# Where the shared expert's tiles stand, a third place for x tiles, logits copied by ScalarE, and a fifth place for gate matrices

## The chip, the core and the metric

The kernel runs on one core of one Trainium2 chip. The metric is the device time in microseconds (us) of one execution; lower is better. Five engines work side by side, each through its own queue of instructions in order: TensorE (PE, with its weight loads as PEld), VectorE (DVE), ScalarE (ACT), GpSimd (POOL) and SyncE (SP, which here only issues DMAs). They wait for each other by semaphores that the kernel sets out by hand. Whatever engine issues a transfer, the core's 16 DMA engines carry it.

## The reference, cut to what matters

The input is two sequences of 1024 tokens, 512 wide. An attention-like layer comes first, then a mixture of 64 experts with a shared expert beside them:

```
x = x + attention(layernorm(x)) @ Wo       # cumulative sum over time, norm over a whole sequence
h = layernorm(x)
logits = h @ w_router.T;  four best of 64 experts per token;  softmax over the four
for each expert (at most C=64 tokens of it):
    y = (silu(h_e @ w_gate[e]) * (h_e @ w_up[e])) @ w_down[e]     # 512 -> 384 -> 512, float32
    combined[tokens of e] += y * weight
combined += (silu(h @ w_sh_gate) * (h @ w_sh_up)) @ w_sh_down     # shared expert, all tokens
out = x + combined
```

Each expert's three float32 matrices are 768 KB (786,432 bytes) each, so the 64 experts bring 151 MB from memory through the DMA engines once.

## The kernel before, in words

The program has two halves. The first takes sequence 0 and then sequence 1, in tiles of 128 tokens (8 a sequence): norm, transposed copy, three projections, scan over time, output projection, residual, second norm, router logits. While the second norm of sequence 0's tiles is made, the first norm of sequence 1's tiles is made beside it: an x tile is loaded by SP into one of two places `xin`, normed, turned by TensorE and split. SP loads these tiles and the tiles for the residual (`ring`, four places) in one order (lines 409 to 420), and before each ring tile it waits for the store of the tile that stood there. In sequence 1's second norm, VectorE copies the router's logits out of PSUM (line 1005, called for tile n-2 after the norm of tile n), and then picks the best experts and builds sorted lists of tokens, a long chain of small VectorE operations.

The second half takes the experts in 32 pairs, two pairs (u = 0 and 1) in each of 16 groups j; pair p = 2j + u. For a pair, tokens are gathered from memory by an indirect DMA of POOL (`xg`, line 605), turned, multiplied with the pair's gate and up matrices (line 1550), silu and product, turned again, multiplied with the down matrices (line 1571), weighted, merged where two experts of the pair share a token (lines 1532 to 1536), and added to the output in memory by an indirect DMA of POOL with addition (line 614). The additions are serial: each waits for the landing of the one before (`added`).

The matrices come through SP's queue, each as two pieces of 384 KB (line 246). A down matrix stands in one of three places; gate and up matrices have a fourth, `extra`. From pair 5 on, SP goes down-of-pair p-2, gate-of-p, up-of-p, and before each it waits until TensorE has finished with what stood in that place (`load_matrix`, `load_down`). What stands behind a waiting transfer in SP's queue waits with it.

The shared expert works on 16 tiles of 128 tokens. The last four of the order (LEAD = 4: tiles 12 to 15 of the token order, kept in SBUF, items 0 to 3 of the shared work) are done around the start: their results are added to the residual x2 in SBUF and stored by `store_late` (line 735), the fourth at the end of group 0. The other twelve (SHARED) are done one to a group, in groups 1 to 12; their turned inputs come back from memory (`xS`), their outputs are gathered in `yS`, three at a time, and added to the output by one POOL DMA (line 627) in groups 3, 6, 9 and 12, in the same serial chain as the pairs' additions. Groups with a shared tile merge in two float32r parts (`y`, `y_low`), the others in whole float32 (`y_whole`).

```
def in_parts(j, u):
    return j + u <= SHARED
BATCHES = range(3, SHARED + 1, 3)
```

Of the kernel before, what the change touches and what calls it, by code (L numbers as in the profile page):

```python
# [25 lines left out]
F32R = mybir.dt.float32r  # L26
# [30 lines left out]
LATE = TOKENS // P - LEAD  # L57


def moe_block(nc, x, wr, wk, wv, wo, decay, gn_w, gn_b, w_router, w_gate, w_up, w_down,  # L60
# [4 lines left out]
    with ExitStack() as ctx:  # L65
# [72 lines left out]
        xin = [tile(f"xin{u}", [P, D], at=xin_at + u * 2048) for u in range(2)]  # L138
# [22 lines left out]
        logits = tile("logits", [P, TILES, E + 4], at=logits_at)  # L161
        top8 = tile("top8", [P, TILES, 8])
# [6 lines left out]
        best = tile("best", [P, C])  # L169
        cand = tile("cand", [E, 2 * C], at=xin_at + 1024)  # L170
# [20 lines left out]
        y, y_low = tile("y", [P, D], F32R, at=ramp_at), tile("y_low", [P, D], F32R, at=logits_at)  # L191
# [4 lines left out]
        y_whole = tile("y_whole", [P, D], at=ramp_at)  # L196
# [14 lines left out]
        def place(p, k):  # L211

            return p % (SLOTS + 1 if k < 2 else SLOTS)

        def uses(p, k):

            return p // (SLOTS + 1 if k < 2 else SLOTS)
# [8 lines left out]

        def in_parts(j, u):

            return j + u <= SHARED

        def gate_up(p, e, k):
            return matrix(p, e, k).rearrange("p (c n) -> p c n", c=KC)
# [6 lines left out]

        def fill_matrix(eng, p, k, experts=range(2)):  # L240

            for e in experts:
                src = (w_gate, w_up, w_down)[k][p * 2 + e].rearrange("(p c) n -> p (c n)", p=P)
                for h in range(PIECES):
                    cols = slice(h * W // PIECES, (h + 1) * W // PIECES)
                    eng.dma_start(matrix(p, e, k)[:, cols], src[:, cols]).then_inc(w_full[k][place(p, k)], 16)  # L246
# [5 lines left out]
        BATCHES = range(3, SHARED + 1, 3)  # L252
# [27 lines left out]
        xin_full, ring_full = sem2("xin_full"), [sem(f"ring_full{i}") for i in range(RING)]  # L280
# [32 lines left out]
        w_full = [[sem(f"w_full{k}_{i}") for i in range(SLOTS + (k < 2))] for k in range(3)]  # L313
# [13 lines left out]
        def xin_place(n):  # L327
# [4 lines left out]
            return xin[n % 2], xin_full[n % 2], 16 * ((n - 4) // 2 + 1 - (n >= TILES))  # L332
# [38 lines left out]
        def _(sp):  # L371
# [38 lines left out]
            for n in range(RING):  # L410
                load_x(n, xc_place)
            for n in range(RING, TILES):
# [1230 lines left out]
```

## Time and profile before

| | us |
|---|---|
| median of 3 runs (lowest, highest) | 733.49 (730.72, 734.45) |
| the profiled execution, its own time | 732.06 |
| its span in the profile | 729.9 |
| TensorE busy in the span | 680.2 (93%) |
| VectorE busy | 332.8 (46%) |
| GpSimd busy | 219.0 (30%) |
| ScalarE busy | 159.7 (22%) |

Durations are taken from the one profiled execution, and are set against its own 732.06 us. The span runs from the first to the last traced instruction. A DMA share is the mean busy share of the 16 DMA engines in a stretch, and can come out a little over 1. In a list of instructions a row is: start in us, busy us, engine, line of the kernel, operation, output<-inputs, and in brackets the idle time of that engine before it and what ended it. "SPq", "POOLq" and "ACTq" are the queues' own issuing of DMAs. Chain rows are the work that ended last, followed back from the end.

### The profile page before, as it was taken

What the parts mean: (1) busy time and instruction counts of PE and PEld (TensorE: products, weight loads), DVE (VectorE), ACT (ScalarE), POOL (GpSimd) and SP (SyncE); (2) the same over time, 40 slices, a digit from 0 to 9 for tenths busy, and PEclk for the clock granted to TensorE, in tenths of its full rate; (3) what the DMA queues carried; (4) which work ended last, traced back from release to release, by engine and by line L of the source; (5) the groups of instructions that cost most, each with busy time, mean ns of one, the idle gap of its engine ahead of it and who ended that gap; (6) DMA issues with size and microseconds to landing.
All of it is one profiled execution on the core that took longest, in us unless ns stands there. A gap on an engine that the chain in (4) does not pass through costs nothing.

```text
span 729.9 us, 9206 instructions
## 1 busy us (share of the span) xinstructions
PE 680.2 (93%) x3229; PEld 411.9 (56%) x3229; DVE 332.8 (46%) x817; ACT 159.7 (22%) x251; POOL 219.0 (30%) x209
## 2 busy tenths in 40 slices
PE   3999999899999998999999999999999999997783
PEld 2687878788787854554554554554554554543330
DVE  5887567648987692233323323323323323322111
ACT  4832215523111221112112112112112112111110
POOL 4637455326646313012121221112121221112101
PEclk9999999589999999999999999999999999999997
DMA  9101006710877888499999999999999999999992
GB/s 324 57 7 53 1 15 237 240 42 1 292 244 270 294 299 278 156 357 378 392 390 375 363 378 376 392 357 379 381 390 377 363 378 374 393 359 378 382 353 33
DMA packets 79996, 202.69 MB, mean 278 GB/s; under 512 B 10403, under 2 KB 10531, under 8 KB 79568
## 3 DMA queue, kind: packets, MB, share of 16 engines
q1 hardware_dynamic: 64160, 169.25, 61.2%
q0 software_dynamic: 8928, 21.33, 12.2%
q10 hardware_dynamic: 6864, 11.54, 4.3%
q8 instruction: 26, 0.43, 0.2%
q14 instruction: 18, 0.15, 0.1%
HBM read 178.66 MB, written 23.59 MB: 277 GB/s over the span
## 4 chain that ended last, share of the span: by engine, by line
PE 65%; SPq 11%; DVE 9%; DMA 3%; issue 2%; POOL 1%; ACT 1%; ACTq 0%; DVEq 0%; POOLq 0%
PE bank L1550 18%; PE bank L1338 12%; SPq L246 11%; PE bank L1571 9%; PE bank L1471 8%; PE bank L1490 5%; PE bank L1360 3%; DMA w_sb<-in_L_ffn_w_up 2%; PE bank L1498 2%; PE bank L1558 1%; DVE key L1045 1%; PE bank L1385 1%; DVE best L1044 1%; PE bank L1461 1%; DVE state L956 1%
## 5 line engine op out<-in xcount | busy, mean ns | idle before, releaser
L614 POOL DMA_INDIRECT out_dram<-ym,midx x32 | 51.3, 1603 | 313.5 <-DVE ym L1235 198.9
L1550 PE MATMUL bank<-w_sb,xT 128*64 128x384 f32 x768 | 129.8, 489 | 6.8 <-DMA w_sb<-in_L_ffn_w_up 4.3
L1338 PE MATMUL bank<-x_hi,w_parts 128*128 128x512 f32 x384 | 123.4, 404 | 4.5 <-DVE x_lo L940 3.2
L1571 PE MATMUL bank<-w_sb,guT 128*64 128x512 f32 x384 | 89.7, 603 | 6.2 <-issue 6.2
L1550 PEld LDWEIGHTS bank<-w_sb,xT 128*64 128x64 f32 x768 | 53.3, 137 | 70.4 <-issue 58.0
L1338 PEld LDWEIGHTS bank<-x_hi,w_parts 128*128 128x128 f32 x384 | 74.6, 195 | 22.1 <-DVE x_lo L940 4.0
L1338 PE MATMUL bank<-x_lo,w_parts 128*128 128x512 f32 x192 | 75.4, 401 | 0.0
L1171 DVE TENSOR_TENSOR gu<-sg,bank 128x384 f32<-128x384 f32 x32 | 17.7, 553 | 124.8 <-issue 117.9
L1471 PE MATMUL bank<-sh_sb,xS 128*128 128x384 f32 x192 | 63.9, 486 | 0.0
L1571 PEld LDWEIGHTS bank<-w_sb,guT 128*64 128x64 f32 x384 | 28.2, 138 | 55.9 <-issue 55.0
L1471 PEld LDWEIGHTS bank<-sh_sb,xS 128*128 128x128 f32 x192 | 35.7, 191 | 22.3
L1490 PE MATMUL bank<-sh_sb,guT 128*128 128x512 f32 x96 | 45.1, 605 | 0.0
L833 ACT ACTIVATE sg<-bank 128x384 f32<-128x384 f32 x32 | 15.7, 491 | 131.9 <-PE bank L1550 131.9
L1550 PE MATMUL bank<-extra,xT 128*64 128x384 f32 x256 | 43.0, 489 | 0.0
L852 ACT ACTIVATE y<-bank,wcol 128x512 fp32r<-128x512 f32 x25 | 17.2, 687 | 116.6 <-PE bank L1571 116.6
L1176 DVE COPY guT<-bank 128x384 f32<-128x384 f32 x32 | 17.7, 554 | 54.1 <-PE bank L1558 54.1
L1338 PEld LDWEIGHTS bank<-x_lo,w_parts 128*128 128x128 f32 x192 | 37.6, 196 | 7.9
L605 POOL DMA_INDIRECT xg<-xw_dram,pair_idx x32 | 31.8, 993 | 28.3 <-DVE pair_idx L1217 10.3
L511 POOL TENSOR_TENSOR v_sb<-v_sb,inv 128x512 f32<-128x512 f32 x16 | 20.8, 1299 | 62.7 <-ACT v_sb L678 61.6
L1235 DVE COPY ym<-bank 128x512 f32<-128x512 f32 x32 | 22.0, 689 | 35.2 <-PE bank L1533 29.6
L487 POOL TENSOR_TENSOR rstd<-var_eps,minus_half 128x1 f32<-128x1 f32 x34 | 21.1, 620 | 45.2 <-DVE var_eps L904 45.2
L1182 DVE TENSOR_TENSOR gu<-sg,bank 128x384 f32<-128x384 f32 x16 | 8.8, 552 | 56.2 <-issue 50.5
(179 smaller groups left out, 954.3 us busy)
## 6 DMA issues: line engine op xcount, KB each, us to landing
w_sb<-in_L_ffn_w_down SPq DMA_DIRECT2D x128, 384.0 KB
w_sb<-in_L_ffn_w_gate SPq DMA_DIRECT2D x96, 384.0 KB
w_sb<-in_L_ffn_w_up SPq DMA_DIRECT2D x96, 384.0 KB
extra<-in_L_ffn_w_gate SPq DMA_DIRECT2D x32, 384.0 KB
extra<-in_L_ffn_w_up SPq DMA_DIRECT2D x32, 384.0 KB
ring<-in_L_attn_x SPq DMA_DIRECT2D x14, 256.0 KB, 3.7
xt_dram<-xwT ACTq DMA_DIRECT2D x12, 256.0 KB, 3.2
xS<-xt_dram SPq DMA_DIRECT2D x12, 256.0 KB
```

The costliest lines, as they stand in the source:

```text
L246: eng.dma_start(matrix(p, e, k)[:, cols], src[:, cols]).then_inc(w_full[k][place(p, k)], 16)
L487: pool.tensor_tensor(rstd[n % 4][:, :], var_eps[n % 4][:, :], minus_half[:, :], ALU.pow).then_inc(rstd_ready, 1)
L511: pool.tensor_tensor(v_sb[u][:, :], v_sb[u][:, :], inv[:, c, t], ALU.mult).then_inc(vscaled, 1)
L605: pool.indirect_dma_start(out=xg[j % 2][u][:, :], out_offset=None, in_=xw_dram[:, :], in_offset=bass.IndirectOffsetOnAxis(ap=pair_idx[:, 2 ...
L614: pool.indirect_dma_start(out=out[:, :], out_offset=bass.IndirectOffsetOnAxis(ap=midx[j % 3][u][:, :], axis=0), in_=ym[u][:, :], in_offset ...
L1235: dve.tensor_copy(ym[u][:, :], pair_bank(j, u)[:, :]).then_inc(ym_ready[u], 1)
L1338: ins = pe.matmul(ps[u][:, :], w, xp, start=(n == 0), stop=(n == len(parts) - 1))
L1360: ins = pe.matmul(ps_y[n % 4][:, :], o, w, start=(m == 0), stop=(m == len(parts) - 1))
L1471: ins = pe.matmul(ps[:, 0:I], xS[t % 2][:, c, :], sh_gu[w][:, c, :], start=(c == 0), stop=(c == KC - 1))
L1490: ins = pe.matmul(ps_d[1][:, :], guT[1][:, c, :], sh_dn[:, c, :], start=(c == 0), stop=(c == IC - 1))
L1550: ins = pe.matmul(ps[e * C:(e + 1) * C, 0:I], xT[:, c, e * C:(e + 1) * C], gate_up(2 * j + u, e, k)[:, c, :], start=(c == 0), stop=(c == K ...
L1571: ins = pe.matmul(pair_bank(j, u)[e * C:(e + 1) * C, :], guT[0][:, c, e * C:(e + 1) * C], down(2 * j + u, e)[:, c, :], start=(c == 0), sto ...
```

## The change

Four things are changed.

1. The twelve shared tiles go from groups 1 to 12 to groups 3 to 14 (FIRST = 3). Groups 1 and 2 have none; the batches of `yS` go from groups 3, 6, 9, 12 to groups 5, 8, 11, 14.
2. x tiles of sequence 1 have three places (the third is half of the old `state` room, so its first load waits for the scan of sequence 0 to end), and each is loaded one place earlier in SP's order.
3. The logits of sequence 1 are copied by ScalarE (`take_logits` there), right after the turned copy of the next tile, and no longer by VectorE.
4. Gate matrices get a fifth place, `spare`, made of four parts of half a matrix. Two parts (expert 0 of the pair) lie over the room of `ramp` and of the lists' work tiles, and may be filled once the token lists are made and the weights are stored; two (expert 1) lie over the residual tiles of the four late tiles, and may be filled when all four are stored (`late_stored` at 64). `y`, `y_low` and `y_whole` move to other room. In the last group the tokens' row of pair 31 is made before that pair's down product.

```diff
-            return p % (SLOTS + 1 if k < 2 else SLOTS)
+            return p % (SLOTS + 2 - k)
+        def has_shared(j):
+            return j == 0 or FIRST <= j < FIRST + SHARED
+        def item(j):
+            return LEAD + j - FIRST if j else TAIL
         def in_parts(j, u):
-            return j + u <= SHARED
+            return has_shared(j + u)
+        def piece(p, e, k, h):
+            if k == 0 and place(p, k) == SLOTS + 1:
+                return spare[e][h][:, :]
+            return matrix(p, e, k)[:, h * W // PIECES:(h + 1) * W // PIECES]
-        BATCHES = range(3, SHARED + 1, 3)
+        BATCHES = range(FIRST + 2, FIRST + SHARED, 3)
@@ SP: a matrix waits for the pair that last stood in its place
-                if k < 2 and p > SLOTS:
-                    sp.wait_ge((g_ready, u_ready)[k][p % 2], p // 2 - 1)
+                last = p - (SLOTS + 2 - k)
+                if k < 2 and last >= 0:
+                    sp.wait_ge((g_ready, u_ready)[k][last % 2], last // 2 + 1)
@@ SP: x tiles
+            sp.wait_ge(out_done, STEPS)
+            load_x(TILES + 2, xin_place)
             for n in range(RING, TILES):
                 sp.wait_ge(xn_ready, TILES + n - RING + 1)
-                load_x(TILES + n - 2, xin_place)
+                load_x(TILES + n - 1, xin_place)
                 sp.wait_ge(x2_stored[n % RING], 16)
                 sp.wait_ge(xw_ready, n - RING + 1)
                 load_x(n, xc_place)
@@ SP: the experts' matrices from pair 4 on
-            for p in range(4, 2 * GROUPS):
-                if p > 4:
-                    load_down(p - 2)
-                if p % 2 and 2 <= (p - 3) // 2 < SHARED:
-                    load_shared_tile((p - 3) // 2)
+            fill_piece(sp, 4, 0, 0, 0)
+            sp.wait_ge(wgt_stored, 16 * SEQS)
+            fill_piece(sp, 4, 0, 0, 1)
+            load_matrix(4, 1)
+            sp.wait_ge(late_stored, 16 * LEAD)
+            for h in range(PIECES):
+                fill_piece(sp, 4, 1, 0, h)
+            for p in range(5, 2 * GROUPS):
+                load_down(p - 2)
+                if p % 2 and 2 <= (p - 1) // 2 - FIRST < SHARED:
+                    load_shared_tile((p - 1) // 2 - FIRST)
                 for k in range(2):
                     load_matrix(p, k)
@@ POOL: the batch of three shared tiles
                 if j in BATCHES:
-                    pool.wait_ge(yS_ready, j + LEAD)
+                    pool.wait_ge(yS_ready, j - FIRST + 1 + LEAD)
@@ ACT: logits of sequence 1
+            def take_logits(n):
+                act.wait_ge(logit_ready, n + 1)
+                if n == TILES:
+                    act.wait_ge(mask_ready, 2)
+                act.activation(logits[:, n % TILES, 0:E], ps_l[n % 2][:, 0:E], ACT.Copy).then_inc(logit_copied, 1)
@@ DVE
                 second_norm(n)
-                if n > TILES + 1:
-                    take_logits(n - 2)
             pick(1, 0)
-            take_logits(2 * TILES - 2)
-            take_logits(2 * TILES - 1)
             pick(1, 1)
@@ PE, last group
                 merge_pair(j, 0)
+                turn_tokens_of_pair(j, 1)
                 if last:
                     down_pair(j, 1)
-                turn_tokens_of_pair(j, 1)
-                if last:
                     merge_pair(j, 1)
```

Order of SP's DMAs before, from the last pieces of pair 3's gate and up matrices on (`extra`k`e`: matrix kind k, expert e; `w_sb`n: place n of three; "x4" is both experts in two pieces each):

```order
L246 DMA extra11_194<-in_L0_ffn_w_up 128x768 x2
L246 DMA extra10_193<-in_L0_ffn_w_up 128x768 x2
L246 DMA w_sb0_195<-in_L0_ffn_w_gate 128x768 x4
L246 DMA w_sb0_195<-in_L0_ffn_w_up 128x768 x4
L246 DMA w_sb0_195<-in_L0_ffn_w_down 128x768 x4
L246 DMA w_sb1_196<-in_L0_ffn_w_gate 128x768 x4
L246 DMA w_sb1_196<-in_L0_ffn_w_up 128x768 x4
L246 DMA w_sb1_196<-in_L0_ffn_w_down 128x768 x4
```

And after, at the same place (`spare`eh: expert e, half h):

```order
L265 DMA extra11_199<-in_L0_ffn_w_up 128x768 x2
L265 DMA extra10_198<-in_L0_ffn_w_up 128x768 x2
L265 DMA spare00_184<-in_L0_ffn_w_gate 128x768
L265 DMA spare01_185<-in_L0_ffn_w_gate 128x768
L265 DMA w_sb0_200<-in_L0_ffn_w_up 128x768 x4
L265 DMA spare10_186<-in_L0_ffn_w_gate 128x768
L265 DMA spare11_187<-in_L0_ffn_w_gate 128x768
L265 DMA w_sb0_200<-in_L0_ffn_w_down 128x768 x4
L265 DMA w_sb0_200<-in_L0_ffn_w_gate 128x768 x4
L265 DMA w_sb1_201<-in_L0_ffn_w_up 128x768 x4
L265 DMA w_sb1_201<-in_L0_ffn_w_down 128x768 x4
```

The gate matrices of pair 4 now go to the spare place, two pieces ahead of that pair's up matrices and two behind them; the down matrices of pair 3, which stood right behind pair 4's up matrices, now stand behind the last two pieces, and so behind the wait for the four late stores.

POOL's DMAs at the end before, from pair 24's addition on (`ym`u: result of pair u of a group; `yS`: three shared tiles; `xg`: gathers):

```order
L614 DMA out_dram<-ym0_182,midx00_155 2048x512
L627 DMA out_dram<-yS_190 128x3x512
L614 DMA out_dram<-ym1_183,midx01_156 2048x512
L605 DMA xg10_200<-xw_dram,pair_idx_153 128x576
L605 DMA xg11_201<-xw_dram,pair_idx_153 128x576
L614 DMA out_dram<-ym0_182,midx10_157 2048x512
L614 DMA out_dram<-ym1_183,midx11_158 2048x512
L614 DMA out_dram<-ym0_182,midx20_159 2048x512
L614 DMA out_dram<-ym1_183,midx21_160 2048x512
L614 DMA out_dram<-ym0_182,midx00_155 2048x512
L614 DMA out_dram<-ym1_183,midx01_156 2048x512
```

And the same stretch after:

```order
L650 DMA out_dram<-ym0_188,midx00_156 2048x512
L650 DMA out_dram<-ym1_189,midx01_157 2048x512
L641 DMA xg10_205<-xw_dram,pair_idx_154 128x576
L641 DMA xg11_206<-xw_dram,pair_idx_154 128x576
L650 DMA out_dram<-ym0_188,midx10_158 2048x512
L650 DMA out_dram<-ym1_189,midx11_159 2048x512
L650 DMA out_dram<-ym0_188,midx20_160 2048x512
L663 DMA out_dram<-yS_195 128x3x512
L650 DMA out_dram<-ym1_189,midx21_161 2048x512
L650 DMA out_dram<-ym0_188,midx00_156 2048x512
L650 DMA out_dram<-ym1_189,midx01_157 2048x512
```

The last batch of shared tiles stood seven additions before the end, and stands three before it now.

VectorE's order in the second norm of sequence 1 before, for one tile (`x_second`: residual, `xw`: normed tile):

```order
L924 TENSOR_SCALAR xw_101<-x_second,mv_116,rstd_124 128x512
L1005 COPY logits<-bank 128x64
L995 SCALAR_TENSOR_TENSOR x_second<-bank,grstd,x_second 128x512
L914 BN_STATS stats<-x_second 128x6
L915 BN_AGGR mv_118<-stats 128x2
L904 TENSOR_SCALAR var_eps_122<-mv_118 128x1
L924 TENSOR_SCALAR xw_102<-x_second,mv_117,rstd_125 128x512
```

And after:

```order
L970 TENSOR_SCALAR xw_102<-x_second,mv_117,rstd_125 128x512
L1041 SCALAR_TENSOR_TENSOR x_second<-bank,grstd,x_second 128x512
L960 BN_STATS stats<-x_second 128x6
L961 BN_AGGR mv_119<-stats 128x2
L950 TENSOR_SCALAR var_eps_123<-mv_119 128x1
L970 TENSOR_SCALAR xw_103<-x_second,mv_118,rstd_126 128x512
```

The copy of the logits, which needs TensorE's router product, no longer stands between a norm and the next residual.

## Rows read from the trace of the kernel before

**Rows 1.** The page: share of the DMA engines in 40 slices of 18.2 us.
```profile
DMA  9101006710877888499999999999999999999992
```

**Rows 2.** Stretches: us, busy of PE, PEld, DVE, ACT, POOL; clock, DMA share, GB/s.
```profile
130.50:151.00 20.50, 18.38 (x68) 15.40 (x69) 10.67 (x32) 9.07 (x13) 6.11 (x12) 0.50 0.67 227
...
296.00:304.00 8.00, 8.00 (x48) 3.40 (x46) 2.13 (x6) 0.49 (x1) 0.00 (x0) 1.00 0.01 2
...
360.00:708.00 348.00, 335.98 (x1671) 165.95 (x1671) 103.09 (x301) 56.97 (x99) 69.34 (x52) 1.00 1.05 378
```

**Rows 3.** The chain that ended last, towards its end: start, us, what.
```profile
597.48 0.79 SPq L246
...
677.78 13.66 DMA w_sb<-in_L_ffn_w_up
```

**Rows 4.** TensorE's instructions: two like groups' starts, and pair 29's down product.
```profile
309.18 5.38 PE L1550 MATMUL bank<-w_sb,xT 128*64 128x384 f32 x32
...
336.55 5.38 PE L1550 MATMUL bank<-w_sb,xT 128*64 128x384 f32 x32
...
696.62 4.49 PE L1571 MATMUL bank<-w_sb,guT 128*64 128x512 f32 x12 [2.33 <-issue]
```

**Rows 5.** The page: the shared expert's products, busy and mean ns of one.
```profile
L1471 PE MATMUL bank<-sh_sb,xS 128*128 128x384 f32 x192 | 63.9, 486 | 0.0
...
L1490 PE MATMUL bank<-sh_sb,guT 128*128 128x512 f32 x96 | 45.1, 605 | 0.0
```

**Rows 6.** SP's queue around group 0: pair 4's gates, pairs 3 and 5 later.
```profile
284.33 1.87 SPq L246 DMA_DIRECT2D w_sb<-in_L_ffn_w_gate  x4
...
304.57 1.75 SPq L246 DMA_DIRECT2D w_sb<-in_L_ffn_w_down  x4
306.37 1.98 SPq L246 DMA_DIRECT2D w_sb<-in_L_ffn_w_gate  x4
```

**Rows 7.** The fourth late store: its issue, and POOL's addition that waits for it.
```profile
310.39 0.34 ACTq L735 DMA_DIRECT2D out_dram<-x_second  x1
...
317.40 1.63 POOL L614 DMA_INDIRECT out_dram<-ym,midx  x1 [26.61 <-DMA out_dram<-x_second]
```

**Rows 8.** The page's DMA issues: engine, count, KB each, median us to landing.
```profile
out_dram<-x_second ACTq DMA_DIRECT2D x8, 256.0 KB, 3.1
```

**Rows 9.** TensorE at the first gathered tile of the experts.
```profile
280.00 0.72 PE L1498 MATMUL bank<-ident,xg 128*128 128x128 f32 x4 [0.78 <-ACT guT L880]
```

**Rows 10.** POOL: around the last batch of shared tiles, and the last additions.
```profile
639.02 1.62 POOL L614 DMA_INDIRECT out_dram<-ym,midx  x1 [8.37 <-DVE ym L1235]
647.47 1.40 POOL L627 DMA_DIRECT2D out_dram<-yS  x1 [6.83 <-issue]
660.40 1.66 POOL L614 DMA_INDIRECT out_dram<-ym,midx  x1 [11.53 <-DVE wcol L1260]
...
688.84 1.56 POOL L614 DMA_INDIRECT out_dram<-ym,midx  x1 [8.94 <-DVE ym L1235]
...
714.70 1.56 POOL L614 DMA_INDIRECT out_dram<-ym,midx  x1 [8.54 <-DVE ym L1235]
721.21 1.55 POOL L614 DMA_INDIRECT out_dram<-ym,midx  x1 [4.95 <-issue]
```

**Rows 11.** VectorE's waits from 102 to 147: us, times, longest.
```profile
DVE stats L914 <- DMA xin<-in_L_attn_x: 2.0, 2, 1.1
```

**Rows 12.** ScalarE's and VectorE's split of sequence 1's x tile 12.
```profile
128.10 0.60 ACT L659 ACTIVATE x_hi<-bank 128x512 fp32r<-128x512 f32 x1 [0.40 <-ACT xwT L721]
...
129.54 0.68 DVE L940 TENSOR_TENSOR x_lo<-bank,x_hi 128x512 fp32r<-128x512 f32 x1
```

**Rows 13.** TensorE's last projection, VectorE's residual of tile 15, its second pick.
```profile
242.20 0.39 PE L1360 MATMUL bank<-wo_hi,out_lo 128*128 128x512 f32 x1
...
246.46 0.74 DVE L995 SCALAR_TENSOR_TENSOR x_second<-bank,grstd,x_second 128x512 f32<-128x512 f32 x1
...
254.06 0.60 DVE L1012 MAX8 top<-logits 128x8 f32<-128x64 f32 x4
```

More of the change, by code:

```diff
@@ L137, in moe_block @@
         xin_at, xn_at, xw_at = room(K4), room(K4), room(K4)
-        xin = [tile(f"xin{u}", [P, D], at=xin_at + u * 2048) for u in range(2)]
+        xin = [tile(f"xin{u}", [P, D], at=a) for u, a in enumerate((xin_at, xin_at + 2048, st_at + 2048))]
         xn = [tile(f"xn{u}", [P, D], at=xn_at + u * 2048) for u in range(2)]
@@ L190, in moe_block @@
         guT = [tile(f"guT{n}", [P, IC, P], at=None if n < 1 else st_at + 2048) for n in range(2)]
-        y, y_low = tile("y", [P, D], F32R, at=ramp_at), tile("y_low", [P, D], F32R, at=logits_at)
+        y_at = xw_at + 2 * I * 4
+        assert y_at + 2 * 2048 <= top8_at and top8_at + W * 2 <= best_end
+        y_whole = tile("y_whole", [P, D], at=y_at)
+        y, y_low = tile("y", [P, D], F32R, at=y_at), tile("y_low", [P, D], F32R, at=y_at + 2048)
+        spare = [[tile(f"spare{e}{h}", [P, W // PIECES], at=a) for h, a in enumerate(places)]
+                 for e, places in enumerate(((ramp_at, top8_at), (inv_at + 8192, inv_at + 8192 + W * 2)))]
         ym = [tile(f"ym{u}", [P, D]) for u in range(2)]
@@ L311, in moe_block @@
         tok_ready, tok_turned, idx_ready = sem("tok_ready"), sem("tok_turned"), sem("idx_ready")
-        w_full = [[sem(f"w_full{k}_{i}") for i in range(SLOTS + (k < 2))] for k in range(3)]
+        w_full = [[sem(f"w_full{k}_{i}") for i in range(SLOTS + 2 - k)] for k in range(3)]
         xg_full = [sem2(f"xg_full{r}") for r in range(2)]
@@ L417, in _ @@
                 load_x(n, xc_place)
-            for n in range(2 * TILES - 2, 2 * TILES):
-                sp.wait_ge(xn_ready, n - 1)
-                load_x(n, xin_place)
+            sp.wait_ge(xn_ready, 2 * TILES - 3)
+            load_x(2 * TILES - 1, xin_place)
             def load_second_rows(c):
@@ L811, in _ @@
                 turned_xw(n)
+                if n > TILES:
+                    take_logits(n - 1)
                 store_residual(n)
@@ L854, in group @@
             def group(j):
-                first, last, shared = j == 0, j == GROUPS - 1, j <= SHARED
+                first, last, shared = j == 0, j == GROUPS - 1, has_shared(j)
                 silu(j, 0)
@@ L1262, in group @@
             def group(j):
-                first, last, shared = j == 0, j == GROUPS - 1, j <= SHARED
+                first, last, shared = j == 0, j == GROUPS - 1, has_shared(j)
                 columns(j, 0)
@@ L1530, in merge_pair @@
                 if in_parts(j, u):
-                    pe.wait_ge(ylow_ready[u], j + 1)
+                    pe.wait_ge(ylow_ready[u], sum(in_parts(i, u) for i in range(j + 1)))
                     pe.matmul(pair_bank(j, u)[:, :], same[u][:, :], y[:, :], start=True, stop=False)
@@ L1575, in group @@
             def group(j):
-                first, last, shared = j == 0, j == GROUPS - 1, j <= SHARED
+                first, last, shared = j == 0, j == GROUPS - 1, has_shared(j)
                 gate_and_up(j, 0)
```

46 lines of the change are left out of this document (27 added, 19 removed).

## The prediction

> **What bounds the kernel now.** I read the page first, then stretches of the span, then the chain that ended last, then the queues. The page's line of DMA shares [rows 1] is the first thing to see: in 22 slices in a row, from about 310 us to 711 us, the 16 DMA engines are 90% busy or more. The stretch from 360 to 708 says how much: DMA share 1.05 at 378 GB/s, with TensorE busy 335.98 of 348 us [rows 2]. So two resources look full at once, and the reader must decide which one sets the end. The chain decides it: up to 597 us it runs over TensorE, from 597.48 on over the issuing of matrices in SP's queue, and from 677.78 over a landing of up matrices [rows 3]. TensorE is ahead of nothing after 597; it has used up the lead that the full places gave it.
>
> A count shows why. A group brings 4 experts x 3 x 786,432 bytes = 9.44 MB of matrices; two gathers of 0.295 MB, two additions of 0.262 MB, one tile of `xS` and a third of a batch of `yS` (0.262 MB each) make it 11.1 MB, which is 29.3 us at 378 GB/s. TensorE needs 27.37 us for a group with a shared tile (309.18 to 336.55 [rows 4]) and some 8 us less without: one tile's products are 63.9/12 + 45.1/16 = 5.3 + 2.8 us [rows 5], so about 19.3 us. The stream of matrices is slower than TensorE in both kinds of groups. Once it runs without a gap, the end is: the time at which it starts to run without a gap, plus its bytes at 378 GB/s, plus what follows the last landings. Where the shared tiles stand changes none of the three by itself; only lost or won DMA time before the stream is full, and the tail, count.
>
> **The fifth gate place and the start of the stream.** Before, SP issues pair 4's gates at 284.33, as soon as pair 0's gate product frees the place, then pair 4's up matrices; the next, pair 3's down matrices, wait for pair 0's down product and go at 304.57, pair 5's gates at 306.37 [rows 6]. Between 296 and 304 the DMA engines do nothing (share 0.01 [rows 2]). From there on the stream is full.
>
> After, half of pair 4's gates (0.79 MB) goes some 10 us earlier, into time in which the engines had room; that gains nothing, since it doesn't bring the full stream forward. Pair 4's up matrices go at about 287 as before. But then SP waits for the four late stores before it issues the other half, and behind that wait stand pair 3's down matrices, pair 5's gates and all that follows. The fourth late store is issued by ScalarE at 310.39 [rows 7]. In the trace POOL's first addition, which waits for the same store, starts at 317.40 [rows 7], but the store then shares the engines with 4.7 MB of matrices. After, it is alone; such stores land 3.1 us after their issue (median of 8 [rows 8]), so at 313.5. That is the bound from below; 317.4, as now, is the one from above. I take 313.5, because the quiet engines are certain.
>
> So the full stream starts at 313.5 instead of 304.57: +8.9 us. It must then also carry the half of pair 4's gates that before was down by then: 0.786 MB / 378 GB/s = +2.1 us. The late store itself (0.262 MB) no longer takes time out of it: -0.7 us. Sum +10.3 us, with bounds +9 and +14. TensorE does not notice at once: pair 2 starts at 309.18 [rows 4], and pair 4 one unshared group later, at about 328.5, while its gates land at about 318. With two unshared groups it then draws faster than the stream supplies, and I expect it to stand waiting for landings from about group 5 on, instead of from group 13 on. Its work is the same; only the place of its idle time moves.
>
> **Gathers beside the extra pieces.** The two early pieces go out right when the token lists are made, beside the first gathers. TensorE's first gathered tile starts at 280.00, 0.78 us after its own work allowed [rows 9], so there is no slack behind the gather. Bounds: 0 and the pieces' whole 0.79 MB, 2.1 us; nearest to the row, which shows the gather and ScalarE's copy arriving together, I take +0.5. The Trainium skill speaks against this placing (DMA: Bandwidth & Descriptors, section Issuing engines are not separate DMA queues): transfers of different issuers run on the same 16 engines and interleave, so another queue is no protection. By that rule the term would be nearer to 2.1 than to 0; no row here shows a gather beside two such pieces.
>
> **The last batch of shared tiles.** POOL's additions are a chain of landings. While the stream is full, an addition issued at 639.02 lets the batch go at 647.47, 8.5 us later; the batch holds the next addition until 660.40, 12.9 us; with idle engines one addition follows the other in 6.5 us (714.70 to 721.21) [rows 10]. Before, the batch of group 12 was long absorbed at the end. After, a batch stands behind the addition of pair 28. That addition starts at 688.84 now; the shared tile's second half (2.8 us [rows 5]) delays its merge: 691.7. Then 8.5 (700.2), 12.9 (713.1, addition of pair 29), 6.5 (719.6), 6.5 (726.1, addition of pair 31), against 721.21 now: +4.9 us on the tail, between 0 (a batch that lands quickly as the stream ends) and +7 (all steps at 8.5). The reordered last merge saves TensorE about a microsecond, which this chain hides.
>
> **Three x places.** VectorE waited 2.0 us for x tiles, twice [rows 11]. Of this only a part comes back: the split of x tile 12 at 129.54 needs ScalarE's copy, which ends at 128.70 [rows 12]. So -0.8 us. Bounds: 0, and a gain through TensorE's clock: from 130.5 to 151 it was granted half (1.2 GHz), with TensorE 18.38 us busy [rows 2]; at full clock that would take up to 9.2 us less. It fell after TensorE had idled between tiles with no projections left to do; VectorE's pace of about 4 us a tile stays, so I expect it to fall again, and take nothing for it.
>
> **Logits on ScalarE.** VectorE's residual of tile 15 starts at 246.46, though its projection ended at 242.59 [rows 13]; the copies of logits, each waiting for a router product, stood in between. Without them it starts up to 3.9 us earlier. ScalarE's seven or eight small copies stand between its turned copies and lie beside TensorE's products. The chain of picking and sorting that starts at 254.06 with the second pick [rows 13] and runs on VectorE to the token lists moves as a whole. Bounds 0 and -3.9; near the row I take -3.4, and lose the rest to turning and routing the last four tiles one after the other.
>
> **Sum.** 10.3 + 0.5 + 4.9 - 0.8 - 3.4 = +11.5 us on the profiled execution's 732.06: 743.5 us (span 741.4). The median of the runs shown is 1.4 us above that execution, which I leave in the range. What a measurement of this kernel can tell from no change is about 0.5%, 3.7 us either way, so 729.8 to 737.2 is the same.
>
> **Rivals.**
>
> 1. Faster, TensorE sets the end. If the 378 GB/s is drawn by TensorE and is not the engines' limit, the late start of the stream is made up, and the idle time of TensorE in the last groups, 348 - 335.98 = 12.0 us [rows 2], goes, since shared tiles now fill it. Span 729.9 - 12.0 - 3.7 (x and logits, less the gathers) + 4.9 = 719.1, time 721. It decides if the DMA rate after 320 rises above 378. For it: TensorE is busy 97% of that stretch. Against: when TensorE starved, after 597, SP's issuing itself was the chain [rows 3], so the queue was full and still gave no more. The Trainium skill would leave it open: DMA: Bandwidth & Descriptors, section Where 436 GB/s comes from, puts the fabric's ceiling at 435 GB/s, which as an estimate would make the 348 us 302. Its page Perfetto Trace Analysis, section Identifying the Most-Contended Engine, also warns of reading the busy share of 16 engines. 7%.
>
> 2. The same: the first half gives more. The clock stays up (half of the bound of 9.2, 4.6 us) and the batch hides (4.9): 743.5 - 9.5 = 734. For it: less waiting for x tiles. Against: VectorE's pace. With smaller parts of both it would end near 737. 17%.
>
> 3. Slower still: the store lands as late as now (+3.9) and the gathers lose 1.6 more: 749. It decides if anything but the two stores of the late tiles uses the engines at 310. 12%.
>
> 4. Slower, by less: the wait for the late stores costs 5 us less, since part of what stood behind it was idle anyway: 738.5. 9%.
>
> The forecast keeps 55%, with its own range 739.5 to 747.5. Faster: rival 1 and a little of 2, 9%. Same: 15%. Slower: the rest, 76%. The range that leaves out at most 2 in 10 reaches down into rival 2 and up to rival 3: 734 to 750.
>
> **What would show it.** DMA share near 0 from about 290 (profile's time, less some 3 us) until after the fourth late store, then 378 GB/s without a gap to the end; SP's down matrices of pair 3 some 7 to 10 us later than 304.57; landing waits of TensorE on L1550's counterpart from group 5 on; POOL's batch behind the fourth addition from the end, and the last addition 5 us later relative to pair 29's down product. VectorE's second pick some 4 us before 254.06. It would be wrong if TensorE waits for no landings in groups 5 to 12, or if the rate goes well above 378 GB/s.

## The result, and the profile after

| | us |
|---|---|
| changed kernel, median of 4 runs (lowest, highest) | 741.32 (739.51, 741.99) |
| kernel before beside it, median of 4 runs (lowest, highest) | 732.46 (730.72, 734.45) |
| ratio, 95% interval | 1.0115 (1.009 to 1.014) |
| profiled execution: its own time, its span | 739.51, 737.7 |

All medians in this document are of fast runs; two runs of the kernel before, at 3876.87 and 797.7 us, are left out.

The change costs 8.9 us where 11.5 were forecast; the interval goes from 6.6 to 10.3 us. The measured time lies in the predicted range. How far the single terms were right is another question, which the experiments answer.

The page's DMA line of the changed kernel, in slices of 18.4 us, answers to [rows 1]:

```profile
DMA  9100007601775995199999999999999999999993
```

The slice with a 1, at about 295 to 313 us, is nearly empty, where before a 4 stood; behind it again an unbroken row of nines. Stretches of the changed kernel, with the columns of [rows 2]:

```profile
130.50:151.00 20.50, 17.37 (x72) 14.18 (x72) 9.13 (x28) 8.20 (x12) 4.91 (x11) 0.67 0.54 192
...
300.00:308.00 8.00, 8.00 (x38) 4.10 (x36) 2.65 (x5) 1.28 (x2) 0.00 (x0) 1.00 0.00 0
308.00:316.00 8.00, 8.00 (x47) 3.29 (x44) 2.71 (x10) 0.79 (x2) 1.64 (x1) 1.00 0.53 170
...
360.00:708.00 348.00, 334.86 (x1637) 166.30 (x1637) 101.99 (x292) 55.77 (x97) 66.03 (x50) 1.00 1.04 380
708.00:738.00 30.00, 10.60 (x47) 3.90 (x43) 3.51 (x8) 1.37 (x2) 4.78 (x3) 0.79 0.50 113
```

From 300 to 308 nothing moves, and the stretch from 360 to 708 goes at 380 GB/s, as before (378). The empty time is that of SP's queue, which answers to [rows 6]:

```profile
285.42 1.75 SPq L265 DMA_DIRECT2D w_sb<-in_L_ffn_w_up  x4
310.97 0.80 SPq L265 DMA_DIRECT2D spare<-in_L_ffn_w_gate  x2
311.82 1.85 SPq L265 DMA_DIRECT2D w_sb<-in_L_ffn_w_down  x4
```

and its cause stands in ScalarE's, where the fourth late store is issued, and in POOL's, where the first addition waits for it ([rows 7]):

```profile
308.90 0.34 ACTq L771 DMA_DIRECT2D out_dram<-x_second  x1
```

```profile
311.91 1.64 POOL L650 DMA_INDIRECT out_dram<-ym,midx  x1 [22.61 <-DMA out_dram<-x_second]
```

The store took 2.1 us, from 308.90 to SP's next issue at 310.97; 3.1 had been taken from [rows 8]. Pair 3's down matrices go at 311.82 instead of 304.57.

TensorE's waits of the changed kernel (line, what ended the wait, total us, times, longest):

```profile
PE bank L1613 <- issue: 15.9, 11, 3.2
...
PE bank L1540 <- DMA xg<-xw_dram,pair_idx: 2.9, 1, 2.9
```

Line 1613 is the down product: TensorE stands before it 11 times, first for 2.4 us before the product at 452.85 us, in group 6. The row names no releaser ("issue"); that these are waits for the down matrices is read from the code, in which this product waits for them and otherwise only for VectorE. The end of the program, in POOL's instructions, answers to [rows 10]:

```profile
695.44 1.55 POOL L650 DMA_INDIRECT out_dram<-ym,midx  x1 [10.94 <-DVE ym L1277]
704.42 1.39 POOL L663 DMA_DIRECT2D out_dram<-yS  x1 [7.43 <-issue]
717.18 1.66 POOL L650 DMA_INDIRECT out_dram<-ym,midx  x1 [11.37 <-DMA out_dram<-yS]
722.86 1.57 POOL L650 DMA_INDIRECT out_dram<-ym,midx  x1 [4.02 <-DMA out_dram<-ym,midx]
729.21 1.55 POOL L650 DMA_INDIRECT out_dram<-ym,midx  x1 [4.79 <-issue]
```

The batch stands between the additions of pairs 28 and 29, as foretold, and the second starts 12.8 us after it (12.9 foretold).

### The profile page after: what moved, and what is told of

Read it like the earlier page. It is cut to its first block and busy times, and to the rows that moved or that the text cites. A ratio compares the mean times of both kernels' runs of the same rounds, so it can differ in the third digit from the quotient of the medians.

```text
span 737.7 us, 9207 instructions
## 1 busy us (share of the span) xinstructions
PE 678.2 (92%) x3229; PEld 407.6 (55%) x3229; DVE 331.2 (45%) x809; ACT 160.9 (22%) x259; POOL 218.7 (30%) x209
## 5 line engine op out<-in xcount | busy, mean ns | idle before, releaser
L1380 PE MATMUL bank<-x_hi,w_parts 128*128 128x512 f32 x384 | 121.6, 399 | 5.6 <-DVE x_lo L986 3.4
L1592 PE MATMUL bank<-w_sb,xT 128*64 128x384 f32 x704 | 121.2, 494 | 1.4 <-ACT xT L873 0.8
L1613 PE MATMUL bank<-w_sb,guT 128*64 128x512 f32 x384 | 90.2, 605 | 16.0 <-issue 15.9
L1592 PEld LDWEIGHTS bank<-w_sb,xT 128*64 128x64 f32 x704 | 49.0, 138 | 61.3 <-issue 56.1
L1613 PEld LDWEIGHTS bank<-w_sb,guT 128*64 128x64 f32 x384 | 28.9, 139 | 66.7 <-issue 66.7
L1513 PEld LDWEIGHTS bank<-sh_sb,xS 128*128 128x128 f32 x192 | 35.7, 191 | 22.3
L641 POOL DMA_INDIRECT xg<-xw_dram,pair_idx x32 | 31.7, 990 | 31.9 <-DVE pair_idx L1259 10.3
L1592 PE MATMUL bank<-extra,xT 128*64 128x384 f32 x224 | 38.5, 489 | 0.3 <-DMA extra<-in_L_ffn_w_up 0.3
## 6 DMA issues: line engine op xcount, KB each, us to landing
w_sb<-in_L_ffn_w_up SPq DMA_DIRECT2D x96, 384.0 KB, 12.9
```

Of the source, the lines that this page charges most:

```text
L641: pool.indirect_dma_start(out=xg[j % 2][u][:, :], out_offset=None, in_=xw_dram[:, :], in_offset=bass.IndirectOffsetOnAxis(ap=pair_idx[:, 2 ...
L1380: ins = pe.matmul(ps[u][:, :], w, xp, start=(n == 0), stop=(n == len(parts) - 1))
L1513: ins = pe.matmul(ps[:, 0:I], xS[t % 2][:, c, :], sh_gu[w][:, c, :], start=(c == 0), stop=(c == KC - 1))
L1592: ins = pe.matmul(ps[e * C:(e + 1) * C, 0:I], xT[:, c, e * C:(e + 1) * C], gate_up(2 * j + u, e, k, c), start=(c == 0), stop=(c == KC - 1))
L1613: ins = pe.matmul(pair_bank(j, u)[e * C:(e + 1) * C, :], guT[0][:, c, e * C:(e + 1) * C], down(2 * j + u, e)[:, c, :], start=(c == 0), sto ...
```

## The experiments

Twelve kernels were run. The first column of the table is the kernel that each starts from.

| from | run | median us (n) | ratio to before, 95% |
|---|---|---|---|
| after | e1_stream_first | 734.41 (12) | 1.0025 (1.0008 to 1.0041) |
| after | e2_shared_from_1 | 740.89 (6) | 1.0112 (1.0087 to 1.0138) |
| after | e3_both | 732.48 (12) | 1.0001 (0.9985 to 1.0017) |
| before | e4_logits_only | 728.54 (9) | 0.9943 (0.9924 to 0.9963) |
| before | e5_x_places_only | 731.16 (12) | 0.9993 (0.9972 to 1.0014) |
| e3_both | e6_gathers_first | 728.93 (12) | 0.9945 (0.9927 to 0.9963) |
| e3_both | e7_fill_idle | 728.44 (10) | 0.9945 (0.9926 to 0.9963) |
| before | e8_before_no_last_batch | 731.34 (12) | 0.9978 (0.9957 to 0.9999) |
| after | e9_after_no_last_batch | 737.95 (9) | 1.006 (1.004 to 1.008) |
| before | e10_plain_batches | 727.85 (8) | 0.9939 (0.9911 to 0.9967) |
| before | e11_front_only | 727.77 (6) | 0.9923 (0.9895 to 0.995) |
| after | e12_less_tensor | 740.40 (6) | 1.0109 (1.008 to 1.0139) |

The kernel before had medians of 732.46, 732.48 and 733.18 beside the three sets: e1 to e4, e5 to e8, e9 to e12. Half an interval is 1.2 to 2.2 us here, so a step of about one microsecond isn't told from none. Four of the kernels leave something out of the result, as is said at each: e8, e9, e10 and e12.

### Where SP waits for the late stores

```diff
             load_matrix(4, 1)
+            load_down(3)
+            for k in range(2):
+                load_matrix(5, k)
             sp.wait_ge(late_stored, 16 * LEAD)
             for h in range(PIECES):
                 fill_piece(sp, 4, 1, 0, h)
-            for p in range(5, 2 * GROUPS):
+            for p in range(6, 2 * GROUPS):
```

> The changed kernel, but pair 3's down matrices and pair 5's gate and up matrices are issued before SP waits for the late stores; the second expert of pair 4's gates follows that wait. Stream theory: the end is the start of the full stream, plus its bytes at 378 to 380 GB/s, plus the tail. The down matrices go at about 303 instead of 310.97, 7.9 us earlier; the late store's 0.7 us is then inside the stream. Expected 741.3 - 7.2 = 734.1, so 1.6 above the kernel before; the DMA rate from 360 to 708 us is unchanged. Rival, the start does not count because TensorE or the chain of additions sets the end: 741, unchanged. Rival, the late store lands late beside the matrices and TensorE stands waiting for pair 4's gates: 736 to 739, with a wait of TensorE for a gate landing near 330 us.

Measured 734.41, 6.9 us less than the changed kernel. SP's queue of this run:

```profile
305.21 1.75 SPq L265 DMA_DIRECT2D w_sb<-in_L_ffn_w_down  x4
307.01 1.97 SPq L265 DMA_DIRECT2D w_sb<-in_L_ffn_w_gate  x4
309.01 2.35 SPq L265 DMA_DIRECT2D w_sb<-in_L_ffn_w_up  x4
317.54 0.80 SPq L265 DMA_DIRECT2D spare<-in_L_ffn_w_gate  x2
```

The stream theory holds, and the largest term is shown: what stood behind the wait was worth 6.9 us. ScalarE issued the fourth late store at 311.03 here, and SP went on at 317.54: beside matrices it is 6.5 us from this store's issue to SP's next, instead of 2.1.

### Does the stream set the end

The shared tiles of groups 3 to 14 are multiplied with the first 128 rows of each shared matrix only; the cut shows the loops, not the lines word for word.

```diff
@@ shared_product: gate and up of the shared expert
-                for c in range(KC):
+                for c in range(1):
@@ down_shared, tiles of groups 3 to 14
-                for c in range(IC):
+                for c in range(1):
```

> The changed kernel, in which the shared tiles of groups 3 to 14 are multiplied with the first 128 rows of each shared matrix only (3 of 11 matrix products a tile are left, so the shared result is wrong); every transfer stays. TensorE has 12 x 5.9 = 70 us less to do. Stream theory: the DMA engines' 380 GB/s set the end, TensorE only waits longer: 740 to 741, with the same rate. Rival, TensorE sets the pace of the stream through the places that it frees: 12 to 70 us less.

Measured 740.40. The stretch from 360 to 708 of this run:

```profile
360.00:708.00 348.00, 290.63 (x1438) 132.68 (x1434) 100.71 (x290) 55.63 (x96) 66.04 (x50) 0.95 1.04 380
```

TensorE is busy 44 us less than in the changed kernel, the rate is the same 380 GB/s, and the time moves by 0.9 us. (Some 70 us of work were taken away; in part the rest grew longer, as the mean granted clock in this stretch is 0.95: over the whole run one product with the down matrices takes 683 ns in the mean, and in the changed kernel 605.) The stream of transfers sets the end; TensorE only waits longer, before its down products 35.7 us (15.9 in the changed kernel) and before gate and up products 23.1:

```profile
PE bank L1614 <- issue: 35.7, 18, 3.8
PE bank L1593 <- DMA w_sb<-in_L_ffn_w_up: 19.8, 13, 3.9
...
PE bank L1593 <- DMA extra<-in_L_ffn_w_up: 3.3, 2, 2.3
```

Rival 1 of the prediction is refuted.

### The place of the shared tiles

```diff
-FIRST = 3
+FIRST = 1
```

> The changed kernel, but the shared tiles stand in groups 1 to 12 again (FIRST = 1); the order of the matrices in SP's queue stays the changed one. Tail theory: the place of the shared tiles counts only through the last batch of yS, which stands between additions 28 and 29 in the changed kernel: 4.9 us less, 736.4. The start of the full stream stays near 311 us. Rival, groups without a shared tile at the front make TensorE draw early and so shared tiles late were themselves a gain or loss of several us: then it stays at 741 (the batch is hidden) or goes to 744 and more (TensorE, ahead of the stream for less long, is starved at the end as before).

> Both edits: matrices ahead of the wait for the late stores, and shared tiles in groups 1 to 12. If the two terms are independent, 741.3 - 7.2 - 4.9 = 729.2, 3.3 us below the kernel before: what is left of the change are the logits on ScalarE, the three x places and the half of pair 4's gates that goes early. If the two terms are one (the last landing of the stream and the chain of additions hide each other), it stays near the better of the two, 734.

Measured 740.89 and 732.48: taking the shared tiles back is worth 0.4 us on the changed kernel (not told from nothing) and 1.9 us where the stream starts early, not 4.9. Two more runs ask where the rest went. The first leaves out the changed kernel's last batch, the second the last batch of the kernel before:

```diff
-        BATCHES = range(FIRST + 2, FIRST + SHARED, 3)
+        BATCHES = range(FIRST + 2, FIRST + SHARED - 1, 3)
```

```diff
-        BATCHES = range(3, SHARED + 1, 3)
+        BATCHES = range(3, SHARED, 3)
```

> The changed kernel, which leaves out its last batch of shared tiles (the one of group 14; three tiles' rows are not added to the output). Theory: the batch stood in the chain of additions at the end (704.42 to 717.18 in the changed kernel's trace), but pair 30's down matrices landed at 713 us, and its addition could not come before 719.5 in any case: without the batch the last addition starts at about 726 instead of 729.21, 3.2 us less, 738.1. Rival, the prediction's tail term in full: 4.9 us less, 736.4. Rival, the batch costs nothing: 741.3.

> The kernel before, which leaves out the fourth and last batch of shared tiles (three tiles' rows are not added to the output). That batch lies inside the full stream, at 647 us. In the traces, stretches of 40 us with a batch in them move 367 to 373 GB/s, those without 385: so a batch costs its own 0.786 MB / 385 GB/s = 2.0 us and some 1.9 us more. Theory: the stream ends 3.9 us earlier, 728.8. Rival, only its bytes count: 730.7. Rival, it is hidden beside a stream that has slack: 732.7.

Measured 737.95 (-3.4 us) and 731.34 (-1.1 us against the runs beside it, interval -3.1 to -0.1). POOL's last instructions without the changed kernel's last batch:

```profile
697.99 1.55 POOL L650 DMA_INDIRECT out_dram<-ym,midx  x1 [10.95 <-DVE ym L1277]
708.07 1.55 POOL L650 DMA_INDIRECT out_dram<-ym,midx  x1 [8.54 <-DVE ym L1277]
720.16 1.55 POOL L650 DMA_INDIRECT out_dram<-ym,midx  x1 [10.54 <-DVE ym L1277]
725.89 1.55 POOL L650 DMA_INDIRECT out_dram<-ym,midx  x1 [4.18 <-DMA out_dram<-ym,midx]
```

The additions of pairs 29 and 30 now wait for VectorE's `ym`, so for the products. The starts of the two executions can't be set against each other as they stand: this one was 2.6 us behind at pair 28's addition, ahead of the batch (697.99 against 695.44), and 2.0 us already at pair 0's (313.90 against 311.91). Counted from pair 28's addition, the last addition starts after 27.90 us here and after 33.77 in the changed kernel, so the batch holds it back by 5.9 us. Not all of it reaches the time. From the start of the last addition to the end of the span it takes 8.49 us in the changed kernel and 10.81 in this run. Three kernels have this longer end, 10.8 to 10.9 us: this one and e8 and e10, the three with fewer than four accumulating batches; the other eleven, the two of the change among them, have 8.4 to 8.7. Why it is longer is not shown: in both kinds the DMA engines have nothing left to do 4.5 us after the addition's start. 5.9 - 2.3 = 3.6 us, and the medians give 3.4.

Nor does the batch stand behind the stream. TensorE's gate and up products of pair 30 and the down products of pairs 30 and 31, in the changed kernel:

```profile
694.05 5.38 PE L1592 MATMUL bank<-w_sb,xT 128*64 128x384 f32 x32
713.25 2.80 PE L1613 MATMUL bank<-w_sb,guT 128*64 128x512 f32 x12 [3.19 <-issue]
718.85 2.79 PE L1613 MATMUL bank<-w_sb,guT 128*64 128x512 f32 x12 [0.62 <-issue]
```

and without the batch:

```profile
696.60 5.38 PE L1592 MATMUL bank<-w_sb,xT 128*64 128x384 f32 x32
713.85 2.79 PE L1613 MATMUL bank<-w_sb,guT 128*64 128x512 f32 x12 [1.33 <-issue]
718.77 2.79 PE L1613 MATMUL bank<-w_sb,guT 128*64 128x512 f32 x12
```

From the first row to the second it takes 19.2 us with the batch and 17.3 without, to the third 24.8 and 22.2. The batch goes out while the last matrices are still on their way, and delays them by 2 to 2.6 us.

In the kernel before, the batch stands in the middle of the stream instead. What part of its cost there is the accumulation is measured by plain batches, which overwrite the output instead of adding to it:

```diff
-                                   yS[:, :, :], accum_op=ALU.add).then_inc(added, ADD)
+                                   yS[:, :, :]).then_inc(added, ADD)
```

> The kernel before, with its four batches of shared tiles as plain writes instead of accumulating ones (the rows of the shared tiles overwrite the output instead of being added to it). A stretch of 40 us with a batch moves 18 GB/s less than one without, 1.9 us a batch. Theory, the accumulation costs the engines this time: 4 x 1.9 = 7.6 us less, 725. Rival, it is the batch's shape and its queue, whatever it does at the destination: 732.5, and the stretches with a batch stay at 367. By the experiment without the last batch (1.6 us less for one batch of 0.786 MB) a batch costs less than its bytes and extra together, so something between, 729, is the rival of both.

Measured 727.85, 5.3 us less for four batches (interval 2.4 to 6.5). Two stretches of the kernel before, of which the first has no batch:

```profile
440.00:480.00 40.00, 40.00 (x203) 19.88 (x201) 12.62 (x36) 7.01 (x12) 6.80 (x5) 1.00 1.04 385
480.00:520.00 40.00, 40.00 (x198) 20.51 (x196) 12.07 (x35) 6.91 (x12) 9.28 (x7) 1.00 1.05 367
```

and the same two with plain batches:

```profile
440.00:480.00 40.00, 40.00 (x201) 19.86 (x199) 12.62 (x36) 7.01 (x12) 6.80 (x5) 1.00 1.04 385
480.00:520.00 40.00, 40.00 (x198) 20.52 (x196) 12.07 (x35) 6.91 (x12) 8.53 (x7) 1.00 1.04 387
```

The dip from 385 to 367 GB/s is gone: it belongs to the accumulation. In the stream a batch costs by these rows 0.786 MB / 385 GB/s = 2.0 us for its bytes and up to 1.9 us for accumulating (1.3 us by the times). Both experiments on the kernel before have the longer end, 10.86 us without the last batch and 10.79 with plain batches, against 8.69. With it added back, one batch in the stream is worth 3.3 us where 3.9 were expected, and the accumulation in four of them 7.4 us where 7.6 were expected, 1.9 us each, as the rates say. These two sums carry the errors of their medians, 1.5 and 2.1 us, and the end is known from one trace of each kernel.

So a batch costs the last addition 5.7 us at the end of the stream (3.4 and 2.3) and 3.3 to 3.9 us in its middle. The difference, 1.8 to 2.4 us, is near the 1.9 us that the place of the shared tiles is worth; that it is all of it is argued, not shown.

### The parts ahead of the stream

The first run moves the logits alone, the second makes three x places alone, the third does both. Their cores:

```diff
@@ DVE
-                if n > TILES + 1:
-                    take_logits(n - 2)
@@ ACT
                 turned_xw(n)
+                take_logits(n - 1)
```

```diff
+            sp.wait_ge(out_done, STEPS)
+            load_x(TILES + 2, xin_place)
...
-                load_x(TILES + n - 2, xin_place)
+                load_x(TILES + n - 1, xin_place)
```

> The kernel before with one part of the change alone: the logits of sequence 1 are copied by ScalarE. Theory: VectorE's chain of picks and rounds starts 3.4 us earlier (second pick at about 250.7 instead of 254.06), and everything behind it, the stream included: 732.5 - 3.4 = 729.1. Rival, the gain is lost by turning and routing the last tiles one after the other, or on the way to the gate product of pair 0, which frees the place of pair 4: 732, with the silu of pair 0 still at 284.3.

> The kernel before with one part of the change alone: three places for x tiles. Theory: VectorE waits less for x tiles, 0.8 us: 732.7 - 0.8 = 731.9. Rival, the higher granted clock seen in the changed kernel's stretch from 130.5 to 151 us (0.67 against 0.50) comes from these places and gives more: 729 to 730. Rival, nothing comes back because the pace of that stretch is VectorE's: 732.7.

> The kernel before with the two parts of the change that act ahead of the stream, logits on ScalarE and three x places, and none of the others. Theory, the two add up: 732.6 - 4.2 - 1.0 = 727.4, below both kernels. Rival, both take back the same waits of VectorE: 728.5, as with the logits alone.

Measured -3.9, -1.3 (interval -2.1 to +1.0, so not told from nothing) and -5.4 us (interval -7.7 to -3.7), each against the runs beside it. The sum of the first two, 5.2, is what the third gives, within the error. This kernel, at 727.77, is faster than both. From 130.5 to 151 us the granted clock was 0.50 with the logits moved, 0.59 with the x places, 0.58 with both, the last two being means over stretches at the lower and the upper level; TensorE's busy time there moved only between 17.66 and 18.04 us.

### The early pieces of pair 4's gates

```diff
+            load_matrix(4, 1)
             fill_piece(sp, 4, 0, 0, 0)
             sp.wait_ge(wgt_stored, 16 * SEQS)
             fill_piece(sp, 4, 0, 0, 1)
-            load_matrix(4, 1)
             load_down(3)
```

> As the kernel with matrices ahead of the late stores and shared tiles from group 1 (e3_both, 732.5), but the two early pieces of pair 4's gates are issued after pair 4's up matrices, behind the first gathers, when the engines run empty. Gather theory: the pieces delayed the first gather, on which TensorE waited 2.9 us in the changed kernel; without them the gate product of pair 0 and all behind it come about 2 us earlier: 730.5. Rival, the wait for the gather is caused by something else (the shorter front: the gathers now start while the up matrices of pair 3 are landing): 732.5, and TensorE waits on the gather as before.

Measured 728.93, 3.6 us less than e3_both. In the changed kernel the first gather, POOL's instruction, and TensorE's wait for it, then its first gate and up products:

```profile
269.83 1.06 POOL L641 DMA_INDIRECT xg<-xw_dram,pair_idx  x1 [10.27 <-DVE pair_idx L1259]
```

```profile
277.05 0.72 PE L1540 MATMUL bank<-ident,xg 128*128 128x128 f32 x4 [2.87 <-DMA xg<-xw_dram,pair_idx]
278.54 6.84 PE L1592 MATMUL bank<-w_sb,xT 128*64 128x384 f32 x32 [0.77 <-ACT xT L873]
```

With the gathers first:

```profile
271.96 1.06 POOL L644 DMA_INDIRECT xg<-xw_dram,pair_idx  x1 [10.28 <-DVE pair_idx L1262]
```

```profile
277.10 0.72 PE L1543 MATMUL bank<-ident,xg 128*128 128x128 f32 x4 [0.78 <-issue]
278.59 5.38 PE L1595 MATMUL bank<-w_sb,xT 128*64 128x384 f32 x32 [0.77 <-ACT xT L876]
```

From the gather's issue to TensorE's turn it takes 7.22 us with the pieces and 5.14 without, 2.1 us. The same 32 products then take 6.84 us against 5.38, another 1.5 us, and the stretches say why:

```profile
278.50:281.50 3.00, 2.96 (x10) 1.24 (x12) 0.00 (x0) 0.00 (x0) 0.94 (x1) 0.50 0.47 144
```

```profile
278.50:281.50 3.00, 2.91 (x18) 1.35 (x20) 0.00 (x0) 0.10 (x2) 0.94 (x1) 1.00 0.69 220
```

After it had idled 2.87 us for the gather, TensorE was granted 1.2 GHz (0.50) for these three microseconds, instead of 2.4 GHz. 2.1 + 1.5 = 3.6 us, the measured step. In e3_both itself, from which this run starts, the same two take 7.26 and 7.08 us, and the sum is 3.8.

### Filling the empty stretch

```diff
+            load_matrix(5, 0)
+            load_matrix(4, 1)
             fill_piece(sp, 4, 0, 0, 0)
             sp.wait_ge(wgt_stored, 16 * SEQS)
             fill_piece(sp, 4, 0, 0, 1)
-            load_matrix(4, 1)
             load_down(3)
-            for k in range(2):
-                load_matrix(5, k)
+            load_matrix(5, 1)
```

> As e3_both (732.5), but SP issues pair 5's gates as soon as pair 0's gate product frees their place, then pair 4's up matrices, then the two early pieces of pair 4's gates, and only then pair 3's down matrices. Stream theory: 1.57 MB more land before the full stream starts near 304 us, in time in which the DMA engines did nothing, 1.57 MB / 378 GB/s = 4.2 us, and the gathers are free of the pieces, 2 us: 732.5 - 6.2 = 726.3. Rival, TensorE becomes the bound or the end is set by the additions: not under 730.

Measured 728.44, 4.0 us less than e3_both, of which the freed gathers alone gave 3.6. The 4.2 us of the filled stretch did not come (0.5 us is left, which is not told from nothing): a miss. SP's queue of this run shows where they went:

```profile
300.32 1.75 SPq L265 DMA_DIRECT2D w_sb<-in_L_ffn_w_down  x4
302.12 2.16 SPq L265 DMA_DIRECT2D w_sb<-in_L_ffn_w_up  x4
311.90 0.80 SPq L265 DMA_DIRECT2D spare<-in_L_ffn_w_gate  x2
312.91 1.75 SPq L265 DMA_DIRECT2D w_sb<-in_L_ffn_w_down  x4
```

and two stretches of it:

```profile
304.00:312.00 8.00, 8.00 (x47) 3.63 (x47) 3.12 (x10) 0.49 (x1) 0.00 (x0) 1.00 0.90 321
312.00:316.00 4.00, 4.00 (x21) 2.27 (x16) 1.48 (x5) 1.28 (x2) 1.63 (x1) 1.00 0.78 237
```

The engines run dry again before 312, since 3.1 MB instead of 4.7 are left to send between 300 and 312. The wait for the late stores (311.90) is only a part of the reason: in e4_logits_only, which has no such wait in SP's queue, pair 4's down matrices also went as late as this,

```profile
281.78 1.77 SPq L246 DMA_DIRECT2D w_sb<-in_L_ffn_w_gate  x4
...
314.62 1.76 SPq L246 DMA_DIRECT2D w_sb<-in_L_ffn_w_down  x4
```

32.8 us after the gate product of pair 0 (281.78), and here 312.91 - 280.07 = 32.8 us after it too. Until pair 1's down product has freed its place, there is no place left to load into. That this is all of the missing 4.2 us is argued from these rows, not shown.

## Why the prediction was right, and where it was not

The forecast, slower by 11.5 us with the restart of the stream as the main term, held: slower by 8.9. The runs give the steps between the kernels, each from medians: the front -5.4, the fifth place with its pieces out of the gathers' way and FIRST = 1 (e6 against e11) +1.2, the pieces beside the gathers +3.6, the shared tiles late +1.9, the late stores ahead of the stream +6.9: +8.2 in all. The step of 1.2 is between two sets of runs and within the error. The first step is taken against the runs of the kernel before beside it (733.18), the result against its own (732.46); that difference of 0.7 closes the gap to 8.9.

1. **What bounds the kernel.** Right. The stream at 380 GB/s sets the end; less work for TensorE changed 0.9 us. The reading that the count of bytes gave was right too, though it took 29.3 us for both kinds of groups; without the shared tile's 0.52 MB it is 27.9, still above TensorE's 19.3.
2. **Restart, +10.3.** The mechanism was right, the size a little too large. The delay by the wait was worth 6.9 instead of 8.9 - 0.7 = 8.2: the store, alone on the engines, took 2.1 us and not 3.1. The 2.1 us for the half of pair 4's gates that goes late can only be compared with the step e11 to e6, 1.2 us, which has an error of about 2.
3. **Gathers beside the early pieces, +0.5.** The term that was furthest off: +3.6 us, outside the bounds of 0 and 2.1. The bound counted the pieces' bytes and left out what TensorE's clock does after an idle stretch. [Rows 9] showed that no slack stood behind the gather; with no slack, the value to take was the upper bound. The Trainium skill (DMA: Bandwidth & Descriptors, section Issuing engines are not separate DMA queues) was right here: by its rule the transfer term was near 2.1, and the rows give 2.1.
4. **Tail, +4.9.** The chain of additions came out as drawn: from pair 28's addition to the last it was to take 34.4 us, and took 33.8. But the price was 1.9 to 0.4 us. The step that failed is the sentence that the place of the shared tiles changes none of start, bytes and rate. The batch that now stands at the end no longer stands in the middle of the stream, where its bytes and their accumulation cost 3.3 to 3.9 us; only the difference to its 5.7 us at the end counts, and the sum took nothing off for it.
5. **Three x places, -0.8, and logits, -3.4.** Measured -1.3 (not told from nothing) and -3.9; the second is at its bound, within the error. VectorE's second pick starts at 249.01 in the changed kernel, 5.0 us earlier, where some 4 were foretold.
6. **Where TensorE would wait.** Waits for landings were foretold from group 5 on. They began in group 6; they are before down products (L1613) rather than before gate and up products.

The errors had opposite signs (gathers +3.1, logits and x -1.2, tail -3.0, restart -2.2). That the sum came nearer than the terms for the gathers and the tail is luck.

Rival 2 (the first half gives 4.6 us more and the batch hides) is true in part: the first half gave 1.2 us more, and most of the tail did not show. Its reason did not hold: the clock rose to 0.67 from 130.5 to 151, yet TensorE's busy time there fell only from 18.38 to 17.37. Rival 3 was right that the gathers cost more, though 2.1 us was still too little, and wrong on the store, which had landed by 310.97 and not at 317. Rival 4 (the wait costs 5 us less) went the right way and too far: the restart cost 2.2 us less than forecast.

## What to carry to other kernels

Where a queue that feeds the bound resource meets a new wait, count everything that stands behind it, and try the order first: here three lines of order were worth 6.9 us and two more 3.6, more than any buffer gained. A stream can be brought forward only as far as there are places to load into; filling the empty stretch ahead of the next release gained 0.5 us here, which is not told from nothing. Whoever moves a transfer out of a full stretch takes its price off there before adding it elsewhere, or the sum counts it twice. And where an engine has no slack behind a transfer, price the wait at its upper bound and add what the engine's clock loses after it.

## What the runs showed of the hardware

- An accumulating write to memory costs the 16 DMA engines more than its bytes: a batch of 0.786 MB takes a stretch of 40 us from 385 to 367 GB/s, and as a plain write it doesn't (387). In time, the accumulation of four of them cost 5.3 us, or 7.4 if the 2.1 us of the longer end are added back.
- The same store of 0.262 MB took 2.1 us from issue to SP's next instruction with idle engines, and 6.5 us beside a queue of matrices.
- From the start of the last addition to the end of the span it took 8.4 to 8.7 us in eleven kernels, and 10.8 to 10.9 in the three with fewer than four accumulating batches. The cause is open.
- A wait of 2.87 us before the first gathered tile was followed by three microseconds at 1.2 GHz, at a cost of 1.5 us for 32 products.
- The stream ran at 380 GB/s over 348 us. The Trainium skill (DMA: Bandwidth & Descriptors, section Where 436 GB/s comes from) says that about 358 GB/s from memory binds such transfers and that 435 is the fabric's ceiling; the 380 measured here, with the kernel on one core, lie between the two. Rival 1 took only the 435 from this section; by its 358, which the trace doesn't bear out either, the section speaks against that rival.
